# Idle turns of the identity on TensorE, one transpose of heads moved past the next tokens, and the last two expert tiles in another order

## What is computed

```
xn = layernorm(x)
q, k, v = xn @ Wq.T, xn @ Wk.T, xn @ Wv.T            # 16 heads of 16
A = tril(taylor_exp(q) . taylor_exp(k))              # 1 + s/4 + s*s/32, s = q.k
y = (A @ v) / (taylor_exp(q) . cumsum(taylor_exp(k)))
attn = y @ Wo.T
top 2 of xn @ Wg, softmax of the two -> combine
ffn = sum_e combine_e * ((silu(xn @ W1_e) * (xn @ W2_e)) @ W3_e)
out = x + attn + ffn
```

## Time and profile before

| | us |
|---|---|
| median of 3 runs | 671.7 |
| lowest and highest | 670.17 and 672.0 |
| the profiled execution | 669.97 |
| its span, first to last instruction | 668.2 |
| TensorE busy in the span | 640.6 (96%) |
| DVE, ACT, POOL busy | 409.9, 341.9, 344.1 |
| mean granted TensorE clock | 0.984 |

### The profile page before, as it was taken

The page is one execution under the profiler, slowest core; times in us unless marked ns, Lnnn a source line. Parts: engine busy times, 40 slices in busy tenths (PEclk is TensorE's granted clock), DMA queues, the critical chain, the costliest instruction groups (busy, mean ns, idle before and its releaser), DMA issues.

```text
span 668.2 us, 16297 instructions
## 1 busy us (share of the span) xinstructions
PE 640.6 (96%) x5351; PEld 493.3 (74%) x5351; DVE 409.9 (61%) x1067; ACT 341.9 (51%) x515; POOL 344.1 (51%) x381
## 2 busy tenths in 40 slices
PE   8799999999999999888999999999999999999994
PEld 6465666666666666546888888888888888888883
DVE  6776878787878585785984445444444544444452
ACT  3577878787877686764653223232322323232231
POOL 3255555546463736463464555555555545455542
PEclk9799999999999999987999999999999999999998
DMA  4643555455434435447533333334342333333332
GB/s 133 143 121 105 123 158 129 151 128 162 81 109 107 124 89 159 113 143 274 179 59 59 51 65 50 61 55 66 51 66 50 57 58 52 64 52 64 52 49 24
DMA packets 37773, 64.05 MB, mean 96 GB/s; under 512 B 8288, under 2 KB 25824, under 8 KB 37696
## 3 DMA queue, kind: packets, MB, share of 16 engines
q0 software_dynamic: 16704, 28.12, 21.4%
q1 hardware_dynamic: 20432, 34.24, 20.1%
q10 hardware_dynamic: 560, 0.66, 0.3%
HBM read 27.72 MB, written 22.68 MB: 75 GB/s over the span
## 4 chain that ended last, share of the span: by engine, by line
PE 87%; DVE 6%; ACT 2%; DMA 2%; issue 2%; ACTq 0%; POOL 0%; POOLq 0%; DVEq 0%
PE banks L1173 30%; PE banks L1194 15%; PE banks L1053 10%; PE banks L1035 8%; PE banks L1073 7%; PE banks L1182 5%; PE banks L1082 4%; PE banks L1117 4%; PE banks L1162 2%; PE banks L1102 1%; ACT T L530 1%; PE banks L1108 1%; DVE xTl L737 1%; PE banks L1091 1%; DMA out<-yo,xw 1%
## 5 line engine op out<-in xcount | busy, mean ns | idle before, releaser
L493 POOL DMA_INDIRECT out<-yo,xw x71 | 112.2, 1581 | 155.7 <-DVE yo L993 102.3
L622 ACT ACTIVATE sTh<-banks 128x512 fp32r<-128x512 f32 x71 | 42.5, 598 | 192.3 <-PE banks L1182 192.3
L473 POOL TENSOR_SCALAR_AFFINE_SELECT T<-T 128x512 f32<-128x512 f32 x128 | 80.6, 641 | 109.9 <-ACT T L536 41.7
L985 DVE TENSOR_TENSOR sTl<-banks,sTh 128x512 fp32r<-128x512 f32 x71 | 49.0, 691 | 118.0 <-ACT sTh L622 118.0
L1173 PE MATMUL banks<-w12h,xgh 128*128 x284 | 118.5, 417 | 0.9 <-DVE xgl L976 0.9
L1173 PE MATMUL banks<-w12l,xgh 128*128 x284 | 112.8, 397 | 0.0
L1173 PE MATMUL banks<-w12h,xgl 128*128 x284 | 112.6, 396 | 0.0
L482 POOL DMA_INDIRECT xg<-xs_scr,glist x71 | 73.4, 1033 | 21.5 <-issue 19.0
L1053 PE MATMUL banks<-T,vau 128*17 128x512 f32 (+3 forms) x1024 | 77.2, 441 | 0.2 <-POOL T L473 0.2
L1035 PE MATMUL banks<-Q,K 32*128 32x256 f32 (+2 forms) x1024 | 71.2, 363 | 6.0 <-DMA K<-Kt 2.8
L464 POOL DMA_INDIRECT xs_scr<-xb,slots x64 | 63.5, 993 | 18.8 <-issue 10.0
(11 more groups left out here) (172 smaller groups left out, 1212.6 us busy)
## 6 DMA issues: line engine op xcount, KB each, us to landing
Q<-Q SPq DMA_DIRECT2D x128, 64.0 KB, 2.3
w12r<-w SPq DMA_DIRECT2D x16, 512.0 KB, 4.8
out<-xa SPq DMA_DIRECT2D x16, 256.0 KB, 2.5
w3r<-w SPq DMA_DIRECT2D x8, 512.0 KB, 7.1
K<-Kt SPq DMA_DIRECT2D x124, 32.0 KB
xa<-x SPq DMA_DIRECT2D x7, 512.0 KB, 4.7
xg<-xs_scr,glist POOLq DMA_INDIRECT x71, 2.9
out<-yo,xw POOLq DMA_INDIRECT x71, 3.8
```

Of the source, the lines that this page charges most:

```text
L473: e.affine_select(out=v, in_=v, pattern=[[0, 4], [1, P]], compare_op=ALU.is_ge, fill=-1.0, base=0, channel_multiplier=-1).then_inc(s["g_mk ...
L493: e.indirect_dma_start(out, bass.IndirectOffsetOnAxis(xw[:, t % 4, NE:NE + 1].bitcast(U32), 0), yo[:, t % 2, :], None, compute_op=ALU.add) ...
L985: e.tensor_tensor(sTl[:], banks[:, 5, :], sTh[:].bitcast(F32), ALU.subtract).then_inc(s["v_st"], 1)
```

## The change

A new kind of step, `f`, turns the identity k times into a bank and releases it itself: 22 turns after FIRST, 9 at the end of slots 29 and 30, 7 within slot 31, then 7, 5 and 4 between the last steps, 63 in all. The step `y(b - 1, 1)` moves from slot 4b, between `c(b, 3)` and `r`, to slot 4b + 1, ahead of `c(b + 1, 0)`, for b = 1 to 6; for b = 7 it stays. Of the last two tiles, TensorE does down(69) ahead of up(70, 1). The programs of DVE, ACT, GpSimd and SyncE have no edit of their own, but the lists of steps that DVE and ACT follow and the banks that the steps get come from the same functions.

```diff
 def slot_b(n):
+    if n == NQ - 1:
+        steps.append(("f", n, 7))
 def slot_c(n):
-        return [("c", b, 3)] + ([("y", b - 1, 1)] if b else []) + [("r", b, 0)]
+        return [("c", b, 3)] + ([("y", b - 1, 1)] if b == LAST else []) + [("r", b, 0)]
     if b == LAST:
-        return [("y", b, 0)] if qd == 3 else []
+        return [("y", b, 0)] if qd == 3 else [("f", n, 9)]
...
-    return ([("c", b + 1, 0)] if qd == 1 else []) + [("v", b + 1, 2 * qd - 2), ("v", b + 1, 2 * qd - 1)]
+    steps = [("y", b - 1, 1)] if b and qd == 1 else []
+    return steps + ([("c", b + 1, 0)] if qd == 1 else []) + [("v", b + 1, 2 * qd - 2), ("v", b + 1, 2 * qd - 1)]
...
-FIRST = (("x", 0, 0), ("x", 0, 1), ("c", 0, 0), ("c", 0, 1), *(("v", 0, i) for i in range(4)))
-END = (("t", LAST, 3), ("y", LAST, 1), ("o", LAST, 0), ("o", LAST, 1))
+FIRST = (("x", 0, 0), ("x", 0, 1), ("c", 0, 0), ("c", 0, 1), *(("v", 0, i) for i in range(4)), ("f", 0, 22))
+END = (("f", NQ, 7), ("t", LAST, 3), ("f", NQ, 5), ("y", LAST, 1), ("f", NQ, 4), ("o", LAST, 0), ("o", LAST, 1))
...
+                elif kind == "f":
+                    for _ in range(k):
+                        i = e.transpose(o[:, 0:P], ident[:], ident[:])
+                    release(i, kind, b, k)
...
             attend(NQ - 1)
+            step("f", NQ, 7)
             step("t", LAST, 3)
+            step("f", NQ, 5)
...
             transpose_g(0)
             step("y", LAST, 1)
+            step("f", NQ, 4)
...
                 transpose_s(t - 1)
+                if t == NT - 1:
+                    down(t - 1)
+                    up(t, 1)
+                    continue
                 if t < NT:
                     up(t, 1)
-                if t + 1 < NT:
                     transpose_g(t + 1)
```

## The result

The changed kernel takes 677.8 us (median of 3 runs, 676.47 to 678.63) where the kernel before takes 671.7: 1.0097 times the time, with a 95% interval of 1.0069 to 1.0125. It is slower by 6.1 us; I had forecast 3.6, and the time lies above the 673.5 to 677 that I gave my own forecast. Its profiled execution has a span of 676.0, 7.8 more than before, and a mean granted clock of 0.992 instead of 0.984: the clock is better and the time worse. A second measurement, beside more runs of the kernel before, gave 1.0093 (1.0076 to 1.011), so the 0.9% stands.

A forecast was written before the change was run, and what follows sets the result against it. TensorE's order was taken as the bound (87% of the span). Turns -3.3, y +5.4 and last tiles +1.5 gave +3.6 us on 671.7: 675.3, own forecast 673.5 to 677 (chance 0.55), eight-in-ten range 669.5 to 678.0.

The forecast's parts named there:

- y's move: Batches: the second v waits for y's bank, released by DVE behind `place_rows`; 0.9 us times 6, 5.4 lost.
- Rivals 1 and 2: At y's move: y fills its hole, 666.6 us, chance 0.10; or y is neutral, 669.9 to 670.6, chance 0.15.
- The turns' gain at the experts: Change to the experts, 304.9 to 311.7 us: turns keep the clock full, 2.8 us won, between 0 and 3.1.
- Rival 3: Wherever turns were added: they do not hold the clock; +6.9 us, 678.6, chance 0.10.
- The start: 21.56 to 28.38 us: turns keep the clock up, 0.5 us won, between 0 and 1.0.
- I take 0 for their own cost: All places of the turns: they stand in existing holes and waits, cost 0, up to 0.5 us in all.
- The DMA queues have nothing new: Said at y's move: SyncE's moves of q and k wait for `c` steps at most 0.1 us later.
- Slots 29 to 31: 291.2 to 294.6 us: TensorE would be 1.7 us earlier but waits for DVE's copy; 0 won.
- The end: Last tiles: TensorE waits for ACT, yo(69) stands behind the last multiply; 1.5 us lost, bounds 0.9 and 1.7.
- My 658.47 for yo(69): Last tiles: forecast start of DVE's yo(69), behind the multiply at 657.86, instead of 656.94.
- rival 4: Batches: the new holes cost clock, a fall in one to three batches; 677.0 to 680.4 us, chance 0.10.
- Rival 2: Batches: y is neutral, bank waits taken up; 669.9 to 670.6 us, 0.7 lower with start won whole, chance 0.15.

The follow-up runs named there:

- y_split_first: The changed kernel, with DVE making y's low part ahead of `place_rows` instead of after: 672.03 us, 1.0004 times the kernel before.
- only_tail: The kernel before with only the new order of the last two tiles: 673.66 us, 1.0031 times the kernel before.
- only_turns: The kernel before with all 63 turns of the identity, y and last tiles unchanged: 667.97 us, 0.9952 times the kernel before.
- end_turns: The kernel before with only the last 16 turns (7, 5 and 4) at the change to the experts: 668.08 us, 0.9988 times the kernel before.
- only_y: The kernel before with only y's move: 677.46 us, 1.0082 times the kernel before.
- first_turns: The kernel before with only the 22 turns at the start: 670.68 us, 1.0022 times the kernel before.
- first_wide: The kernel before with 10 products of 512 columns at the start, in place of the 22 turns: 668.74 us, 0.9987 times the kernel before.
- tail_dve: The kernel before with the new order of the last tiles, and DVE weighing tile 69 ahead of its last multiply: 669.88 us, 1.0006 times the kernel before.
- slot_turns: The kernel before with only the turns of slots 29 to 31 (9, 9 and 7): 669.28 us, 1.0000 times the kernel before.
- first_short: The kernel before with 22 products of 16 columns at the start, in place of the 22 turns: 671.46 us, 1.0021 times the kernel before.
- all_wide: The kernel before with all turns, the 22 at the start replaced by 10 wide products: 667.40 us, 0.9970 times the kernel before.

## Why the prediction was right and wrong

**y's move: right in its mechanism and nearly in its size.** The forecast was 0.92 a batch from y's bank, which is handed back behind `place_rows`. Measured is 0.94 up to the end of the wait, and 0.10 for the refilling of the stream, which I had left out. y_split_first, which moves nothing but that hand-over, shows the cause. Rivals 1 and 2 fall: y filled no hole, and it was not neutral. Of the 6.98 from slot 4 to slot 28 some 0.7 more lies outside the two slots of this wait. It is not y's, and not of the change at all: only_tail, which is the kernel before up to its last tiles, loses 1.4 over the same slots and only_turns 0.9, and the second profile of the changed kernel (after_again) loses 6.3, six times 1.04. It differs between executions; its cause is open.

**The turns' gain at the experts: right for that execution, high for the mean.** The forecast was 2.8, the profile of the changed kernel shows 2.81, and end_turns alone is worth 0.8 in its timed runs. The profiles offer a reason. From the first expert product to the wait for xgl the six profiles with turns there take 11.97 to 12.04 us. The three without them in which the clock fell for 6.8 us (before, only_y, only_tail) take 14.7 to 14.8, and the two in which it fell for 3.4 take 12.9 and 13.5 (first_turns, first_wide). But tail_dve, slot_turns and first_short, which have no turns there either, had no fall at the change and take 11.99 to 12.00. So the turns are worth 2.8 against a fall of 6.8 us and nothing where none comes. A saving that is read from one profile with a fall is an upper end, not the mean.

**Do turns hold the clock? All together, yes; not each group by itself.** Rival 3 falls. The six profiles with turns at the change to the experts (changed, after_again, only_turns, y_split_first, end_turns, all_wide) have the full clock there; before, only_y, only_tail, first_turns and first_wide fell to 1.2 GHz, and three had no fall without turns. More telling is the whole stretch from 280 to 320 us. The five with turns in the slots and at the change have no fall in it; each of the nine others has at least one, end_turns (at 297.5) and slot_turns (at 296.9) too. At the start it fell in four of the five profiles with the 22 turns. The Trainium skill ("TensorE: Matmul & The Clock Gate", Part 4) says that transposes do not count as busy for the clock. Where the page and these rows differ, the rows decide: with these transposes of 128 by 128 in fp32 the clock rose and was held.

**The start: wrong, in sign.** The sentences that failed are "I take 0 for their own cost" and, further on, "The DMA queues have nothing new". I had counted the data moves, found none added, and left out that TensorE's instructions are themselves fetched by DMA. Twenty-two more of them shift the fetch into the eight K moves that end the hole: the first scores start 1.2 us late and slot 4 is 1.5 late, where I had 0.5 won, a miss of 2.0. The 22 turns cost 1.5 us by themselves. I had also said that TensorE would be idle anyway until the K landed; that hid the turns' own length, but not their fetch.

**Slots 29 to 31: 0 forecast, -0.3 read, 0.0 timed.** Under it a second case of the same thing shows. In the seven profiles in which TensorE has 19 or more added instructions ahead of slot 30, and in none of the other seven (0 to 10 added), one of the eight K issues there takes 0.99 to 1.85 us where all others take 0.59. In six of the seven TensorE then waits for a K: 1.03 in only_turns, 2.29 in first_turns, 1.47 in all_wide. The SyncE issues of that place in the kernel before, in only_turns and in first_turns:

```profile
L317 SPq DMA_DIRECT2D K<-Kt x8: 587/589/596, 277.6 to 282.1; - x8
```

```profile
L320 SPq DMA_DIRECT2D K<-Kt x8: 587/589/1739, 277.3 to 282.8; - x8
```

```profile
L318 SPq DMA_DIRECT2D K<-Kt x8: 588/589/1848, 278.7 to 284.3; - x8
```

In each of those seven a fetch of 16 KB starts within 0.35 us of that long issue; in the seven others every fetch of this stretch lies before the first of the eight issues or behind the last. This was read and not tried: no kernel moved that fetch alone.

**The end: right in its mechanism, short by 0.6.** The step mis-sized is the 1.5 for the last tiles; only_tail measured 2.1 by its profile and by its runs. Against the lag of 5.60 at transpose_s(69), the multiply came 2.6 later, where I had 2.4, and yo(69) 2.0 later (7.62 - 5.60), where I had 1.5. My 658.47 for yo(69) can't be: the multiply is 0.69 long, so one that starts at 657.86 ends at 658.55, and the changed kernel's rows have 0.17 more between its end and yo. Of the 0.5 between the two, half is this slip and half is the multiply's own lateness.

**New holes in the batches (rival 4): no.** From 64 to 250 us the granted clock is 1.00 in the changed kernel and in only_y, with both waits in every batch.

**The range.** My 673.5 to 677 is not what the bounds of the terms give. Taken all at their low ends they come to -2.5 us, at their high ends to +8.8, so 669.2 to 680.5. Rival 2's "0.7 lower" should by the bounds of the start be 0.5.

**The sum.** The parts timed alone give +5.5, -3.2 and +2.1, +4.4 us in all. The whole change measured +6.2 (0.93%, 0.76 to 1.10). The 1.8 between them is 0.28% of the time, and the half widths of the four intervals, combined as the root of their squares' sum, are 0.35%, so it cannot be told from zero. In the changed kernel's two profiled executions the clock fell at the start in spite of the turns, and in only_turns it did not. Whether that is the rest is open. What turned my 3.6 into a measured 6.2 is, by the rows, the start (2.0), y's refill (0.6) and the tail (0.6 to 0.9), with 0.7 more in the batches that is not the change's. Together with the 3.6 that is 7.5 to 7.8, where the two profiles are 7.8 apart; the medians lie 1.6 below that.

## What to carry to other kernels

Before moving a step on the bound engine, write down whose bank it takes and whose bank the steps behind it take in turn, and then look where in the other engine's list the release of that bank stands: the move cost 1.04 us a batch through a release, and putting that one release earlier gave most of it back. Filler instructions can be cheap by their time and dear by their number. In a stretch whose end is a DMA's, use few long ones, and look at the instruction queue's row and at the longest issue of each queue afterwards. A gain from the clock read in one profile should be weighed by how often the clock falls there in other executions.

## What the runs showed of the hardware that I had not expected

- **A fetch of instructions holds up the issue of small moves.** With the 16 KB fetch among them one issue on ACT's queue took 1.76 to 1.85 us, where the median is 0.67 to 0.68, and one on SyncE's 1.41 to 1.49 instead of 0.59. This is seen at the start in the changed kernel and in first_short, and not there in before and first_wide, whose fetches lie elsewhere. It isn't new with the change: in all 14 profiles together 80 of the K issues took over 0.8 us, six of them in the kernel before, and 79 of these 80 overlap a fetch on queue q8. Not every issue that overlaps one is long.
- **Twenty-two small instructions move that fetch; ten large ones of the same total length do not.** It starts at 17.4 to 18.0 us in the profiles with 22 more, and at 21.0 to 21.8 in those with ten or none. 22 products of 16 columns do it as 22 transposes do.
- **The clock falls in different places in one program's family.** Leaving out the fall at the end of each profile, the kernel before fell at 21.6, 291.2 and 304.9 us, end_turns at 21.0 and 297.5, all_wide at 23.2 alone, first_wide at 305.0 alone, and only_turns nowhere. A fall lasted 3.4, 6.8 or, once, 10.2 us.
- **The first product after a wait is longer**: 0.39 us instead of 0.28 for 264 columns (L1086), and the scores behind it are 0.10 later.
